# Causal attention on TensorE: two heads side by side on the 64-row halves, six products in place of nine, the mask as a matmul of its own

## The reference

```python
attn = jnp.einsum('bhqd,bhkd->bhqk', q, k) / jnp.sqrt(hd)
alibi = -slopes[None, :, None, None] * (Tt - 1 - jnp.arange(Tt))[None, None, None, :]
attn = jnp.where(causal, attn + alibi, jnp.finfo(x.dtype).min)
p = jax.nn.softmax(attn, axis=-1)
out = jnp.einsum('bhqk,bhkd->bqhd', p, v).reshape(Bb, Tt, C)
```

## Time and profile before

| | us |
|---|---|
| median of 3 runs | 1278.57 (1277.38 to 1294.37) |
| span of the profiled execution | 1285.2 |
| busy in it: TensorE, VectorE, ScalarE, GpSimd | 1010.8, 804.3, 546.7, 487.5 |
| mean granted clock of TensorE | 0.875 |

### The profile page before, as it was taken

The page is one execution under the profiler, slowest core; times in us unless marked ns, Lnnn a source line. Parts: engine busy times, 40 slices in busy tenths (PEclk is TensorE's granted clock), DMA queues, the critical chain, the costliest instruction groups (busy, mean ns, idle before and its releaser), DMA issues. The chain is left out here.

```text
span 1285.2 us, 20321 instructions
## 1 busy us (share of the span) xinstructions
PE 1010.8 (79%) x6768; PEld 603.9 (47%) x6768; DVE 804.3 (63%) x2127; ACT 546.7 (43%) x878; POOL 487.5 (38%) x484
## 2 busy tenths in 40 slices
PE   5872119952589999999899998898888989998882
PEld 3661017741134434444335443343257868884551
DVE  4667860132686888788987888768627533555654
ACT  1431004422126656656566654464563433432141
POOL 3101145525504610352016420232434444556776
PEclk9885558985559999999999998887899999999995
DMA  4225403421321311131122232153137755642122
GB/s 115 66 66 166 73 11 95 120 64 36 106 75 32 110 43 44 35 107 41 41 67 88 88 84 66 42 156 120 46 89 213 209 159 158 175 129 58 46 76 64
DMA packets 113122, 114.88 MB, mean 89 GB/s; under 512 B 17813, under 2 KB 95253, under 8 KB 109781
## 3 DMA queue, kind: packets, MB, share of 16 engines
q1 hardware_dynamic: 73830, 74.07, 20.9%
q0 software_dynamic: 12048, 25.71, 7.2%
q10 hardware_dynamic: 27144, 13.83, 3.7%
HBM read 67.94 MB, written 41.94 MB: 85 GB/s over the span
## 5 line engine op out<-in xcount | busy, mean ns | idle before, releaser
L2159 DVE TENSOR_REDUCE maxima<-psum 128x1 f32<-128x512 f32 (+4 forms) x624 | 384.6, 642 | 106.1 <-PE psum L1974 54.9
L2097 ACT ACTIVATE probs<-psum 128x1024 f32<-128x1024 f32 (+3 forms) x384 | 299.0, 809 | 262.6 <-PE psum L1993 199.3
L2007 PE MATMUL psum<-probs,v_wide 128*32 128x512 f32 (+3 forms) x1536 | 173.7, 526 | 0.0
L1970 PE MATMUL psum<-ka,qa 75*128 75x512 bf16 (+3 forms) x440 | 146.6, 345 | 22.6 <-DVE maxima L2159 16.6
L1481 POOL DMA_INDIRECT sorted<-x_rows,to_row x76 | 75.4, 992 | 213.4 <-ACT probs L2097 118.4
L2518 ACT ACTIVATE g_silu<-psum 128x512 f32<-128x512 f32 x80 | 47.8, 597 | 177.1 <-PE psum L2424 105.0
L1989 PE MATMUL psum<-qa,ka 78*128 78x512 bf16 (+3 forms) x440 | 117.2, 332 | 4.7 <-DMA qa<-max_parts 2.4
L1407 POOL DMA_INDIRECT w_gu<-expert_out,to_row x64 | 65.8, 1029 | 137.0 <-ACT probs L2097 95.7
L2424 PE MATMUL psum<-w_gu,g_xT 128*128 x384 | 97.1, 396 | 9.1 <-DVE g_h L2594 5.5
L1970 PEld LDWEIGHTS psum<-ka,qa 75*128 75x128 bf16 x440 | 42.8, 99 | 123.8 <-DVE maxima L2159 104.0
L116 POOL DMA_INDIRECT f_got<-expert_out,dense x64 | 64.1, 1002 | 64.6 <-DMA f_got<-expert_out,dense 44.1
(11 more groups left out here) (333 smaller groups left out, 1823.3 us busy)
## 6 DMA issues: line engine op xcount, KB each, us to landing
g_rows<-sorted SPq DMA_DIRECT2D x192, 64.0 KB
expert_out<-g_y ACTq DMA_DIRECT2D x48, 256.0 KB, 2.8
qa<-q_steps SPq DMA_DIRECT2D x30, 192.0 KB
ka<-k_steps SPq DMA_DIRECT2D x10, 576.0 KB
w<-in_W SPq DMA_DIRECT2D x16, 256.0 KB, 3.0
w_gu<-in_gu SPq DMA_DIRECT2D x4, 1024.0 KB, 10.4
sorted<-blank SPq DMA_DIRECT2D x54, 64.0 KB
q_steps<-w_gu SPq DMA_DIRECT2D x12, 256.0 KB
```

The costliest lines, as they stand in the source:

```text
L1970: mm = pe.matmul(bank[:, h * width:h * width + plain], qa[b][0:ROWS_MAX, h0 + h, qt * P:(qt + 1) * P], ka[b][0:ROWS_MAX, h0 + h, seg * HAL ...
L2007: mm = pe.matmul(B[OUT][32 * h:32 * (h + 1), q0 - c * HALF:HALF], v_wide[s.buf][:, j, h, PAD * (1 - c):PAD * (1 - c) + 32], probs[k % PRIN ...
L2097: act.activation(probs[k % PRING][:, 2 * pair:2 * pair + 2, 0:w], PS[:, 2 * pair:2 * pair + 2, 0:w], ACT.Exp).then_inc(exps, 1)
L2159: dve.tensor_reduce(maxima[:, seg, h0:h0 + heads, qt], bank[:, 0:heads * width].rearrange("p (h k) -> p h k", h=heads), AX.X, ALU.max).the ...
```

## The change

- `qa` and `ka` hold two groups of rows, in partitions 0 to 63 and 64 to 127 (`SIDES`, `SIDE`), each for two of the step's four heads (`PER_SIDE`). Heads 0 and 1 are on the first side, 2 and 3 on the second.
- Six of the nine products of parts are kept (`PRODUCTS`), so that a side needs 48 + 3 + 3 = 54 rows. The three smallest products are dropped.
- The mask rows leave the operands. They are 43 rows in a small tile `G.mask`, once on each side, and the diagonal block gets its mask by a matmul of its own, 128 columns wide, that starts the accumulation; the block's scores are added by the same matmul as the rest of the unit.
- A unit holds heads of one side; successive units alternate between the sides. The one unit of four heads (query tile 4) becomes two. A step has 41 units, before 40.
- A pair of scores is one head of each side, in the PSUM banks 0 and 1 or 2 and 3 (`score_bank`).
- Order in a slot: two units, both pairs of scores, the other units, P·V.
- The operands no longer lie in `w_down`; the load of `w_down` loses its wait. Loads become 12 + 2 DMAs a step (before 4 + 2), direct loads 12 on each of two queues (before 9).

```diff
-            heads = max(1, min(GH, HALF // width))
-            if qt == 0:
-                heads = 2
-            units += [(qt, seg, h, heads, width) for h in range(0, GH, heads)]
+            heads = min(PER_SIDE, HALF // width)
+            units += [(qt, seg, side * PER_SIDE + h, heads, width)
+                      for h in range(0, PER_SIDE, heads) for side in range(SIDES)]
...
+    for side in range(SIDES):
+        at = side * SIDE
+        for part, first, copies in ((0, 0, 3), (1, 3, 2), (2, 5, 1)):
+            rows = slice(at + first * HD, at + (first + copies) * HD)
+            sp.dma_start(G.qa[s.buf][rows].rearrange("r h n -> r (h n)"),
+                         q[side, part][None, :, :].to_broadcast([copies, HD] + wide)).then_inc(G.here[s.buf], 16)
+            sp.dma_start(G.ka[s.buf][rows].rearrange("r h n -> r (h n)"), k[side, 0:copies]).then_inc(G.here[s.buf], 16)
...
                         for h in range(heads):
-                            if plain:
-                                mm = pe.matmul(bank[:, h * width:h * width + plain], qa[b][0:ROWS_MAX, h0 + h, qt * P:(qt + 1) * P],
-                                               ka[b][0:ROWS_MAX, h0 + h, seg * HALF:seg * HALF + plain],
-                                               start=(h == 0), stop=True, skip_group_check=True)
                             if diagonal:
-                                mm = pe.matmul(bank[:, h * width + plain:(h + 1) * width],
-                                               qa[b][0:ROWS_DIAGONAL, h0 + h, qt * P:(qt + 1) * P],
-                                               ka[b][0:ROWS_DIAGONAL, h0 + h, qt * P:(qt + 1) * P],
-                                               start=(h == 0 and plain == 0), stop=True, skip_group_check=True)
+                                pe.matmul(bank[:, (h + 1) * width - P:(h + 1) * width], G.mask[at:at + MASK_ROWS, 0, :],
+                                          G.mask[at:at + MASK_ROWS, 1, :], start=(h == 0), stop=False, skip_group_check=True)
+                            mm = pe.matmul(bank[:, h * width:(h + 1) * width],
+                                           qa[b][at:at + ROWS_MAX, (h0 + h) % PER_SIDE, qt * P:(qt + 1) * P],
+                                           ka[b][at:at + ROWS_MAX, (h0 + h) % PER_SIDE, seg * HALF:seg * HALF + width],
+                                           start=(h == 0 and not diagonal), stop=True, skip_group_check=True)
...
+                    diagonal = q0 == j * P
+                    heads = (pair, pair + PER_SIDE)
+                    if diagonal:
+                        for h in heads:
+                            at = side_of(h)
+                            pe.matmul(B[score_bank(h)][:, 0:P], G.mask[at:at + MASK_ROWS, 1, :], G.mask[at:at + MASK_ROWS, 0, :],
+                                      start=True, stop=False, skip_group_check=True)
+                    for h in heads:
+                        at = side_of(h)
+                        mm = pe.matmul(B[score_bank(h)][:, 0:(c + 1) * HALF - q0],
+                                       ka[s.buf][at:at + ROWS_ALL, h % PER_SIDE, j * P:(j + 1) * P],
+                                       qa[s.buf][at:at + ROWS_ALL, h % PER_SIDE, q0:(c + 1) * HALF],
+                                       start=not diagonal, stop=True, skip_group_check=True)
...
-                        apart = [slot[:len(slot) // 3], slot[len(slot) // 3:2 * len(slot) // 3], slot[2 * len(slot) // 3:]]
+                        apart = [slot[:2], [], slot[2:]]
                         for part, pair in zip(apart, (0, 1, None)):
```

More of the change, by code:

```diff
@@ L51 @@
 MASK_GROUP = 3
[L52 to L53 removed]
+MASK_ROWS = -(-P // MASK_GROUP)
 SCORE_SCALE = float(1 / np.sqrt(np.float32(HD)))
@@ L1038, in next, with loads_until @@
         return Step(self.n + by, b % BUFS, self.used + b // BUFS)
[L1041 removed]
+LOADS = SIDES * (2 * 3 + 1) * 16
+DIRECT_LOADS = SIDES * 2 * len(PRODUCTS)
+def loads_until(s):
+    return s.used * LOADS + LOADS + ((DIRECT_LOADS - SIDES * 2 * 3) * 16 if s.buf == 0 else 0)
 def emit_load_alibi(sp, G, I, s):
[L1046 to L1047 removed]
+    for side in range(SIDES):
+        at = side * SIDE + ALIBI_AT
+        sp.dma_start(G.ka[s.buf][at:at + 3].rearrange("r h n -> r (h n)"), I["c_alibi"][s.n, side]).then_inc(G.here[s.buf], 16)
@@ L1050, in emit_load @@
 def emit_load(sp, G, I, s):
[L1052 to L1061, removed]
+    q = G.q_steps[s.n:s.n + 1].rearrange("o j (u d p) n -> u j (o d) (p n)", u=SIDES, d=HD)
@@ new lines, in emit_load @@
+    k = G.k_steps[s.n:s.n + 1].rearrange("o j (u d p) n -> u j (o d) (p n)", u=SIDES, d=HD)
+    wide = [PER_SIDE * SEQ]
+    for side in range(SIDES):
+        at = side * SIDE
[4 more added lines that the diff above has]
+            sp.dma_start(G.ka[s.buf][rows].rearrange("r h n -> r (h n)"), k[side, 0:copies]).then_inc(G.here[s.buf], 16)
@@ L1064, in emit_fixed_rows @@
 def emit_fixed_rows(sp, G, I):
     for b in range(BUFS):
[L1067 to L1070, removed]
+        for operand, first in ((G.qa[b], ALIBI_AT), (G.ka[b], MAX_AT)):
+            for side in range(SIDES):
+                at = side * SIDE + first
+                sp.dma_start(operand[at:at + 3].rearrange("r h n -> r (h n)"), I["c_ones"]).then_inc(G.ones_here, 16)
@@ L1071, in emit_fixed_rows @@
+    for which in range(2):
+        for side in range(SIDES):
+            sp.dma_start(G.mask[side * SIDE:side * SIDE + MASK_ROWS, which, :], I["c_mask"][which]).then_inc(G.mask_rows_here, 16)
     for n in range(2):
         emit_load_alibi(sp, G, I, Step(n, n, 0))
[L1075 to L1081, removed]
 def emit_load_direct(sp, G, Q, which, part):
[L1086 to L1090, removed]
+    for side in range(SIDES):
+        heads = Q.parts[which][side * SIDES * HD:(side + 1) * SIDES * HD, part, :]
+        for block, parts in enumerate(PRODUCTS):
+            if parts[which] == part:
+                at = side * SIDE + block * HD
+                sp.dma_start((G.qa, G.ka)[which][0][at:at + HD], heads).then_inc(G.here[0], 16)
@@ L2809, in build @@
             A = Mem(nc, operands)
-            in_room = [G.w_down[:, u * GH * SEQ // 2:(u + 1) * GH * SEQ // 2].bitcast(bf16).rearrange("p (h n) -> p h n", h=GH)
-                       for u in range(2)]
-            G.qa = [in_room[0] if b == EARLIEST_FREE else A.sb(f"qa{b}", [P, GH, SEQ], bf16) for b in range(BUFS)]
-            G.ka = [in_room[1] if b == EARLIEST_FREE else A.sb(f"ka{b}", [P, GH, SEQ], bf16) for b in range(BUFS)]
+            G.qa, G.ka = [[A.sb(f"{x}a{b}", [P, PER_SIDE, SEQ], bf16) for b in range(BUFS)] for x in "qk"]
+            G.mask = A.sb("mask", [P, 2, P], bf16)
             with ExitStack() as first:
```

45 lines of the change are left out of this document (20 added, 25 removed).

## The result

The changed kernel takes 1311.33 us (1308.11 to 1317.01, four runs), the kernel before 1286.47 in the runs beside it (1277.38 to 1295.04): **1.0193 of before, 95% interval 1.0125 to 1.0262**. That is slower by just under the 2% that count as a change here, inside the predicted range, 28 us above the predicted time. The profiled execution has a span of 1310.0 us against 1285.2.

A forecast was written before the change was run, and what follows sets the result against it. Neither engine alone was taken to bound: TensorE and VectorE pass two PSUM banks back and forth. +4 − 6 − 1 − 3 + 2 + 8 = +4 us gave 1289 for the profiled span, 1283 us in the runs, range 1250 to 1319.

The forecast's parts named there:

- What bounds: Attention steps: TensorE and VectorE pass two PSUM banks; TensorE stands 119 us for reduces, VectorE 95 us for units.
- parts 1 and 2: Attention slots: score sides run at once; the third unit waits for the first reduce, some 0.5 us of TensorE idle.
- the walk: Twelve slots of a step timed with rules from the trace: 31.2 us against 30.8 at full clock.
- the sum: All terms for the whole kernel: +4 us, 1289 for the profiled span, 1283 in the runs.
- Part 3: Separate mask matmuls and one more unit: +0.4 us a step, +4 us over steps 1 to 11 (−5 to +10).
- Part 4: Stretches at half clock and last step: steps 12 to 14 −6 us, step 0 −1, last step −3.
- Part 5: DMA: direct loads before the first step +2 us (0 to +3); a step's extra loads nothing.
- Part 6: Clock in steps 1 to 11: fewer columns in the same time bring some falls, +8 us (0 to +42).
- the +8: Steps 1 to 11: 28 us of half clock taken, each costing 0.29 of it, +8 us.
- The freed stream: Faster rival: full banks remove half of VectorE's idle 66 + 28 us, −50 us, 1229 us; chance 0.16.
- The serial sides: Slower rival: the sides don't run at once, 33.0 us a step, +33 over fifteen steps, 1314 us; chance 0.11.
- The clock's rival: Slower rival: TensorE's gaps ahead of P·V lower the clock in steps 1 to 11, +42 us, 1317 us; chance 0.19.

The follow-up runs named there:

- e5: Kernel before, VectorE's reduce of units of 256 or more columns a head reading only the later half: 0.9519 of before, 1230 us.
- e6: Kernel before with the new order in a slot alone (two units, both pairs of scores, the other units, P·V): 0.9875 of before.
- e8: Kernel before with VectorE's half reduce and the new order in a slot: 0.9597 of before.
- e3: Changed kernel with every pair of scores computed twice into the same banks: 1.0113 of before, 1303 us.
- e4: Changed kernel, VectorE's reduce of units of 256 or more columns a head reading only the later half: 0.9758 of before, 1258 us.
- e11: Kernel before with six products instead of nine (those of k's third part left out), columns and order kept: 1.246 of before, 1600.18 us.
- e12: Changed kernel with both pairs of heads on rows 0 to 63, so no two of their matmuls run at once: 1.2086 of before, 1558 us.
- e9: Changed kernel with each pair of scores and each two successive units on one side; sides still ran at once: 1.0251 of before.

## Why the prediction was right or wrong

**What bounds, and parts 1 and 2: right.** The sides run at once, the third unit waits for the first reduce (0.22 us for the 0.5 forecast; the slot shown begins with a reduce of 384 elements, which is over sooner), VectorE idles around P·V as before. One row was misread: the 119 us are idle time of the weight loads, and the matmuls themselves waited 20 us for that cause. At clock 1.00 in both profiles, steps 3 to 6 differ by +0.3, +1.2, +0.8 and 0.0 us; the walk said +0.4. The half reduces confirm that VectorE's reduce is on the path, on which the sum hung: step 3 at 27.4 in the changed kernel (27.2 expected) and 29.1 in the kernel before (28.4 expected).

**Part 3: open in its size.** What doubling the units' masks costs in the whole is not told from none. The 2.3 us of loss ahead of step 0, at half clock in both kernels, were not in the sum; the doubled masks added another 1.8 there, so masks are the likely cause.

**Part 4: half right.** Step 0 (−1 predicted, −0.8) and the last step (−3, −2.3; 21.7 us for "about 21") came. Steps 12 to 14 gave −0.9 for −6, while the stretch at half clock grew (clock 0.76 for 0.81); how much the walk at half clock is off there, no run separates.

**Part 5: the direct loads were under-priced, and the "nothing" of the step loads failed in one step.** Of the +4.5 us up to the first reduce, 2.7 had passed before the first copy of the operands was issued, and 1.8 lie between that copy and the reduce, near the +2. But both figures are chance in part. The first copy is issued anywhere from 316.6 to 322.4 us in the profiles of the changed kernel and of its variants here; and from this copy to the first reduce the kernel before takes 15.5 to 15.9 us in e5, e6 and e8 (17.9 in its own profile), the changed kernel and its variants 19.7 to 20.9. So the direct loads cost some 4 to 5 us. For the step loads the prediction asked only whether SyncE has time to issue them. It had; but in step 1 the maxima rows landed late behind the packets of earlier copies, 1.72 us of idle TensorE on the chain that the prediction had called near.

**Part 6: right sign, wrong reason, half the size.** The step that failed is the +8. It priced 28 us of half clock at 0.29 us each; there were 66 (403 us at 0.918, unrounded). Of the +23.7 in steps 1 to 11 some 4 to 6 are the walk (4 forecast, 6 by the four steps at clock 1.00) and 2 to 4 the late maxima rows (step 1 grew by 3.8 us, and in e3, at clock 0.99, by as much). The remaining 14 to 18 over 62 us of new half clock are 0.22 to 0.29 each, so the price about held and the amount didn't. The reason given was fewer columns in the same time. But e4 passes the same matmuls in 8% less time at the same clock, and e11 has all of before's columns and falls to 0.65: what the prediction had not priced is the six products, that is, the matmuls' height (the rows of the contraction). With all heads on rows 0 to 63, one matmul at a time, the change cost 21% (e12), and the six products alone cost the kernel before 25% (e11); laying two sides beside each other returned nearly all of that. The result of +2% is the difference of two large effects that no step of mine contained, so that the measured time lies as near the forecast as it does is luck. Whether the clock follows the rows at work at the same moment, or whether the upper rows are used at all, e12 doesn't separate, since both differ there; e9, which was to do so, ran its sides at once. Nor does any run show that the height is the reason for all of the smaller fall, from 1.00 to 0.92, in the changed kernel itself.

**Rivals.** The freed stream did not feed VectorE: step 3 is not under 29 us. The serial sides are refuted by the timeline. The clock's rival had the right cause in name, at 0.92 and not at 0.81, and its 1317 us lie nearer to the 1311 measured than my 1283. Its mechanism, gaps ahead of P·V, is not the main one: the old order in the changed kernel has a lower clock (0.88), and e11 and e12 hardly leave TensorE idle and stand at 0.65. That gaps have a part in the changed kernel's 0.92 is not excluded, since e3, which brings the clock back, also fills them. The Trainium skill's rule on PSUM-queue depth-cycling ("TensorE: Matmul & The Clock Gate", section on the second failure mode), by which that rival would have come in full, is not what decides here: the kernel before cycles through two banks as well and stands at 1.00 in steps 1 to 11.

## What to carry to other kernels

Cutting a contraction from 78 to 54 rows saved no time on the array here: at clock 1.00 two score matmuls of 78 rows and 512 columns take 0.60 us, and four of 54 rows, one after the other, 1.02 (e12), about 0.21 us for each one more in both. And it took the clock with it: look at the granted clock of every stretch before a change that makes TensorE's work smaller, and try the smaller operands alone first. Doubling the rate of one engine in an exchange over two banks moved nothing while the other engine's reduce set when a bank was free; halving the reduce was worth 63 us in the kernel before (26 of them in steps 12 to 14, where the clock rose as well), the doubled rate of the scores nothing. And a moved block of DMAs is costed by the one landing behind it that has no slack, not by the time that the queue needs to issue it.

## What the runs showed that I had not expected

- Fewer rows in the same matmuls, with the same columns and order: granted clock 1.00 to 0.65 in steps 1 to 11, and 316 us more in the whole. Computing the scores twice in the changed kernel raised it from 0.92 to 0.99, and the kernel was no slower for it (1303 against 1311 us, intervals overlap).
- In e9 matmuls start ahead of their turn. The order there is two score matmuls of one side, then two of the other, and only the second of each pair signals ScalarE. In the four that took 0.59 us the two without a signal start together and the two with one 218 ns later: the first of the second pair ran beside the first of the first pair. Of the 135 starts within 30 ns in steps 1 to 11, 127 pair matmuls in this way. ScalarE's exponential of the first pair began 0.69 us after the first score's start there, 0.48 in the changed kernel, which agrees: the second matmul of the first pair was the late one.
- A shorter reduce on VectorE also brought back the clock: in e5, steps 12 to 14 of the kernel before went from 0.81 to 0.98, and two fifths of e5's gain lie there (26 of 63 us, in 3 of 16 steps).
